# A transformer layer on eight cores: projection matmuls interleaved with attention at four per key block instead of two

## The reference

```python
x: (4, 4096, 1024) f32; 16 heads of 64; hidden 3072
Q, K, V = x Wq^T, x Wk^T, x Wv^T          # per head
S = Q K^T / 8, causal mask
O = softmax(S) V                          # blocked over keys, online in the reference
x = layernorm(x + O Wo^T)
h = silu(x Wg^T / 127) * (x Wu^T / 127)   # int weights
x = layernorm(x + h Wd^T / 127)
```

## Time and profile before

| | us |
|---|---|
| median of 3 runs | 2137.75 |
| lowest and highest | 2129.0, 2195.58 |
| the profiled execution | 2132.75 |
| its span, slowest core (core 5) | 2131.7 |
| spans of the other cores | 2101.8 to 2123.6 |
| granted TensorE clock, mean by core | 0.861 to 0.870 |

### The profile page before, as it was taken

One profiled execution on the slowest core, in us unless ns is written; L12 is line 12 of the kernel. 1 busy time (PEld: TensorE's weight loads), 2 busy tenths in 40 slices (PEclk: granted clock), 3 DMA queues, 4 the chain that ended last, 5 costly groups with the idle time before them and its releaser, 6 DMA issues. The chain is left out here.

```text
span 2131.7 us, 22780 instructions; the slowest of 8 cores (2101.8 to 2131.7 us)
## 1 busy us (share of the span) xinstructions
PE 1649.6 (77%) x7240; PEld 603.1 (28%) x7240; DVE 613.1 (29%) x1436; ACT 825.4 (39%) x999; POOL 183.9 (9%) x221
## 2 busy tenths in 40 slices
PE   3857989678888678888667775677899889998872
PEld 1512222212223222223111111222344334443320
DVE  1333132252332252322431222264311112111224
ACT  0025768156775067773237664133111011112012
POOL 1010000100000200000000000001122011221000
PEclk9967999869999679999558787787999999999985
DMA  7691122642123702215100000424679666777622
GB/s 101 108 128 21 21 41 39 93 59 40 21 41 55 102 14 41 40 21 81 21 1 1 1 1 2 121 72 45 60 70 86 58 65 58 72 72 68 93 55 79
DMA packets 224112, 115.31 MB, mean 54 GB/s; under 512 B 152030, under 2 KB 215520, under 8 KB 224000
## 3 DMA queue, kind: packets, MB, share of 16 engines
q0 software_dynamic: 215104, 96.94, 37.4%
q1 hardware_dynamic: 8896, 16.91, 2.3%
HBM read 201.66 MB, written 8.65 MB: 99 GB/s over the span
## 5 line engine op out<-in xcount | busy, mean ns | idle before, releaser
L415 ACT ACTIVATE pt<-sp,cbias 128x1024 bf16<-128x1024 f32 (+3 forms) x640 | 620.4, 986 | 271.3 <-PE sp L403 257.9
L443 PE MATMUL op<-pt,vbuf 128*65 128x512 bf16 (+3 forms) x1280 | 375.0, 377 | 136.6 <-DVE pt L424 60.8
L398 PE MATMUL sp<-qbuf,kbuf 64*128 64x512 bf16 (+3 forms) x640 | 239.9, 384 | 2.1 <-DVE cbias L324 2.1
L403 PE MATMUL sp<-qbuf,kbuf 64*128 64x512 bf16 (+3 forms) x640 | 240.1, 384 | 0.0
L899 PE MATMUL dps<-hbuf,wdd 128*128 128x512 bf16 x768 | 178.8, 391 | 35.6 <-DVE y L910 34.4
L841 PE MATMUL gps<-x1b,wgb 128*128 128x512 bf16 x768 | 185.0, 384 | 22.5 <-DVE x1b L809 13.0
L443 PEld LDWEIGHTS op<-pt,vbuf 128*65 128x65 bf16 x1280 | 109.4, 116 | 298.6 <-issue 269.4
L850 PE MATMUL ups<-x1b,wub 128*128 128x512 bf16 x768 | 183.8, 383 | 6.8 <-DVE hbuf L862 6.8
L226 PE MATMUL pp<-xstg,wkb 128*128 128x512 bf16 x512 | 153.4, 410 | 45.3 <-DMA xstg<-xfm 39.8
L240 PE MATMUL pp<-wvb,xstg 128*128 128x256 bf16 x1024 | 174.1, 281 | 0.8
L858 ACT ACTIVATE sgb<-gps 128x512 bf16<-128x512 f32 x96 | 57.3, 597 | 300.6 <-PE gps L841 291.2
(11 more groups left out here) (83 smaller groups left out, 1219.7 us busy)
## 6 DMA issues: line engine op xcount, KB each, us to landing
xstg<-xfm POOLq DMA_DIRECT2D x32, 1024.0 KB, 9.2
xstg<-xq POOLq DMA_DIRECT2D x16, 1024.0 KB, 9.5
wgb<-wgT POOLq DMA_DIRECT2D x48, 256.0 KB, 4.7
wub<-wuT POOLq DMA_DIRECT2D x48, 256.0 KB, 5.5
wdd<-wdT POOLq DMA_DIRECT2D x16, 768.0 KB, 10.1
xres<-xq SPq DMA_DIRECT2D x32, 256.0 KB, 3.1
yout<-y SPq DMA_DIRECT2D x4, 2048.0 KB, 6.9
wqb<-wqT POOLq DMA_DIRECT2D x4, 512.0 KB, 10.6
```

The source lines that it names most:

```text
L398: nc.tensor.matmul(sp[buf][:, js * 128: 512], kbuf[pb][0:64, hp * T + kb * 128: hp * T + kb * 128 + 128], qbuf[pb][0:64, hp * TOWN + qbase ...
L403: s_s.inc(nc.tensor.matmul(sp[buf][:, 512 + js * 128: 1024], kbuf[pb][64:128, hp * T + kb * 128: hp * T + kb * 128 + 128], qbuf[pb][64:128 ...
L415: s_exp.inc(nc.scalar.activation(pview, sview, AF.Exp, bias=cbias[pb][:, 0:1]))
L443: lastpv = nc.tensor.matmul(ops[hl][:, js * 128: 512], vbuf[pb][:, kb * VGW + (2 * hp + hl) * 65: kb * VGW + (2 * hp + hl) * 65 + 65], pt[ ...
```

## The change

The number of generator steps taken in each slot goes from 2 to 4. Nothing else differs; every instruction is still there, in another order.

```diff
@@ -499,7 +499,7 @@
             if p >= 1:
                 parts.append(norm_gen(p - 1))
             filler = chaing(*parts) if parts else None
-            filler = attention_pass(p, filler, rate=2)
+            filler = attention_pass(p, filler, rate=4)
             if filler is not None:
                 for _ in filler:
                     pass
```

## The result

The changed kernel takes 2079.62 us (median of 10), the kernel before 2140.79 (median of 10); the ratio is 0.9743, with a 95% interval of 0.9715 to 0.9771, so it is 2.6% faster. The profiled execution of the changed kernel took 2079.08 us. Where a sentence on core 5 compares both kernels, its spans are 2076.3 after and 2131.7 before. Some executions of an eight-core program are a few per cent longer whatever the kernel; ratios leave them out, and where a time is called "about", a median holds such executions, and the ratio times 2139, the middle of the medians of the kernel before in the experiments (2138.0 to 2140.6), stands in its place.

The account below looks back on a forecast made before the run. Slots with K or Q fillers were taken as bound by PE, the others by ACT. Passes 0 to 2 with their tails gain 11.3, 7.3 and 6.7 us, pass 3 loses 1.5: -24, 2110 us said, range 2076 to 2144.

Parts of the forecast that it names:

- rival of a larger gain: Fillers in PE's idle time keep the clock full, diagonal V slots stay 1.05, no x waits: -60, 2073 us; chance 0.24.
- The tail: Between passes: 2.9 us of DVE copies, 25.1 of the bound c, up to 1 waiting for late loads; together 29.
- Pass 3: Last attention pass, only the normalisation as filler: two more yields in its first slot put PV behind the wait, +1.5 us.
- The normalisation: Slots 112 to 114 of passes 1 and 2: 7.3 us wait, 23.3 in all against 22.9 in the tail; no gain.
- Bank starts: Each bank's first slot, where PE waits 3.1 us for DVE's copies: two more fillers are hidden there at present price.
- Full V slots: Non-diagonal slots with V fillers at rate 4: 1.335 us each, now bound by PE; 34 a pass counted.
- Diagonal slots: Last 8 slots of each bank at rate 4: K or Q 1.47 us, V 1.18 with 0.1 added for mask waits.
- Loss at the half clock: Passes take 13 us more than their count, mostly stretches at 1.2 GHz after idle bank starts; left as it is.
- x tiles: Key tile loads hidden; the first Q tile's load makes PE wait about 3 us a pass, between 0 and 14.
- theory A: Gain beyond the forecast is half-clock time PE no longer loses, since fillers fill the idle time at bank starts.
- rival of displaced work: The 128 yields cost 23 us in either place; diagonal V slots cost 1.35: 2127 to 2145 us; chance 0.21.
- The slower one: Granted clock in the dense 112 slots falls to a mean near 0.80: +48 us, 2181; chance 0.08.

Follow-up runs that it names:

- e11: e7 with three x buffers in place of two, and the normalisation issued early in parts, its write and reloads by SP; 1935 us, ratio 0.9046.
- e4: Kernel before (2 fillers a slot), but 8 fillers in each bank's first slot; 2081 us, ratio 0.9748 to the kernel before.
- e2: Changed kernel with 6 fillers a slot in place of 4; about 2135 us, ratio 0.998 to the kernel before.
- e7: Changed kernel with fillers given out by PE time per slot (full 0.32 us, diagonal 0.46, bank's first 2.2) instead of by number; 2005 us, ratio 0.9379.
- e9: e5 with the normalisation's write and reloads issued by SP instead of POOL; about 2060 us, ratio 0.9635 to the kernel before.
- e5: Changed kernel with the normalisation taken apart: transfers in the second key tile, broadcasts singly, one every 8 steps; 2086 us, ratio 0.9766 to the kernel before.
- e8: e7 with the normalisation taken apart, still on POOL, broadcasts one every 16 steps, allowances 2.4 and 0.52; 2011 us, ratio 0.9419.

## Why the forecast was right or wrong, step by step

The direction was right and the time, 2079.6, is within the stated range, near its low end. The likeliest case, -24 us and 2092 to 2125, did not come, and the forecast had put 0.66 on a change within 2% and only 0.26 on a faster kernel. The measured -55 is close to the rival of a larger gain (-60), so the range holds the result by that rival's share in it, not by the sum. By its steps, on core 5:

- *The tail*, 28 to 29 us: right, 27.8 to 28.1. The 1 us wait for late loads did not come.
- *Pass 3*, +1.5: right, +1.1.
- *The normalisation*: right. PE waits 6.73 us where 7.3 was said, and bank 2 with it takes 59.1 us in pass 1 against 35.6 in pass 0, 23.5 where 23.3 was said. Moved as a block it gains nothing; e11 shows that it gains when taken apart.
- *Bank starts*: right. From the end of one bank's last product to the next bank's first are 3.1 us as before (238.74 to 241.83), with four fillers hidden in them.
- *Full K slots*: right, 1.72. *Full V slots*: 1.30 instead of 1.335, which is 34 x 0.04 = 1.4 us a pass.
- *Diagonal slots*: the term that was mis-sized. Bank 2 of the first pair takes 35.0 us at clock 1.00; without 7 x 1.72 + 1.29 + 8 x 1.30 + 2.9 = 26.6 there are 8.4 for 8 V slots, 1.05 each, what a slot costs at rate 2, not 1.18. Bank 3 gives in the same way 9.7 for 4 K and 4 V slots, so a K slot is 1.38, not 1.47. Together 27 x 0.13 + 19 x 0.09 = 5.2 a pass. 1.05 is also the forecast's own PE work of such a slot, 0.60 and the 0.45 measured for four V fillers, so no wait for the mask was left on top; the 0.1 put on top had no row behind it.
- *Loss at the half clock*, left at 13 us a pass: wrong in place, and too high. With the terms above the count of a pass is 233.6 - 1.4 - 5.2 = 227.0; pass 0 took 239.5, so 12.5 are left, 3.5 of them waits for x. So 9 us against the 13 kept. This 9 is a remainder, not a measured time. The stretches at the half clock add up to about as much as before, 29.4 us of pass 0 against 30.5 (granted mean 0.93 in both); what changed is where they stand. Banks 2 and 3 of the first pair have none now. Bank 3 of the second pair, without fillers, has 10 us of them and takes 40.2 us, where the count of its bare slots is 24 x 1.16 + 8 x 1.05 + 2.9 = 39.1: in slots bound by ACT they cost 1 us. The largest piece of the 9 is in the bank where the Q tiles begin, 31.9 - 24.2 - 2.86 = 4.8 us. The forecast also priced the loss of the kernel before twice, at 13 us in its sum and at 7 to 8 in the rival of a larger gain; e4 puts it near 10.
- *x tiles*, 3 us: 2.86 + 0.65 = 3.5 measured in pass 0. As a wait right. The bank takes 31.9 us where the count with the new terms gives 24.2; the rest is the half clock that the point above has, of which 3.4 us follow the wait and 6.8 the bank's start.

Pass 0 by terms: 6.6 less from the slots, 3.9 less from the clock, 0.5 more for x, 10.0 in all. The three passes were 10.0, 10.6 and 8.6 us shorter than said (249.5, 273.0, 270.8), and each tail 1 us: 32 us on these stages of core 5, against the 30 between 2109 and 2079. So theory A alone, which put all of it on the clock, was too strong for the changed kernel: more than half (6.6 of the 10.0 in pass 0) is diagonal slots and V fillers, as far as the two banks read stand for all. The clock is decisive for the kernel before, where e4 wins it back.

The rival of displaced work failed at its first step, diagonal V slots of 1.35. The slower one needed a mean clock near 0.80 in the dense stretch; it was 1.00 in two of its banks and 0.84 in the worst. Of the larger gain's three items, diagonal V slots at 1.05 came (3.5 us a pass), the clock came in part (3.9 of 5 to 6), and the waits for x, which it had at nothing, stayed. That its total was nearly met is in part luck: K slots in the diagonal and the V fillers made up for the x tiles.

The forecast set a third level of the clock aside by the earlier trace rows. The profiled execution of the changed kernel agrees with it; that of e2 does not, as the last section shows.

## What to carry to other kernels

Filler work should be given out by the time that each slot has to spare, not by number: here 0.3 us in a slot bound by ACT, more in a diagonal one, over 2 us at a bank's start, and with that a pass that holds its whole projection took less time than one that held five sevenths of it. Before a change of rate is costed, read from one bank at full clock what its slots take, and price time at the half clock apart, with the place that causes it. No run gave a fixed number to the slots and more to the bank starts at a rate that leaves no tail, so how much of e7's gain is the filling of bank starts and how much the pacing inside them is not shown. A small chain of transfers moved earlier belongs on a queue where no large load stands behind it.

## What the runs showed of the hardware

- In twelve of the thirteen profiled executions TensorE's granted clock took only its two levels, 1.2 and 2.4 GHz, with all eight cores in dense matmuls: banks at 1.00 for 35.0 and 46.7 us, PE busy 95 and 96%. The thirteenth, that of e2, has a third level. Windows of e2: core 0, then the same stretch on core 5.
```profile
170.00:290.00 120.00, 117.08 (x607) 53.98 (x607) 36.62 (x96) 60.75 (x61) 6.99 (x8) 0.81 0.40 63
...
170.00:290.00 120.00, 111.17 (x663) 53.81 (x662) 40.72 (x108) 65.52 (x66) 7.86 (x9) 0.98 0.47 73
```
  There cores 0 and 1 were granted 0.81 in this stretch, cores 2 and 3 in a later one (from 1850 to 1970 us), cores 4 to 7 never. Eight matmuls of 512 columns took 2.10 us on core 3 at 0.81 and 1.73 on core 4 at 1.00. The Trainium skill (TensorE: Matmul & The Clock Gate, Part 1) expects this level, 13/16, for a die of which three cores or more run dense matmuls. The trace of e2 agrees with the level; the other twelve, with the same load, do not show it, so the load alone does not bring it here.
- At the bank starts of passes 0 to 2 on core 5, idle time of 2.0 to 2.8 us was followed by half clock at 18 of 21 in the kernel before and at 10 of 15 in the changed one; with 0.7 to 1.6 us idle it was at none of 23 (6 in the changed kernel, 17 in e4). The same page (Why this matters for your kernels) names idle of PE between bursts of matmuls as what brings the lower level back; at these starts the trace agrees in kind, though not every time. The stretch of e9 in the next point it does not explain: in the 20 us before it PE was idle for 0.89 us at most.
- The f32 broadcasts, which use 2 of 128 rows, ran at half clock for 13.99 us back to back. In e9 core 5 stayed at 0.50 for 27.3 us in which PE was busy for 26.15, eight such matmuls among them, while core 7 kept 1.00 over most of the same instructions. So here a busy PE did not bring the full level back. How densely the broadcasts stand may matter: in e5 and e9, with one every 8 steps, between 1 and 8 of a pass's 16 such matmuls ran at half clock on every core; in e8 and e11, with one every 16 steps, none of 512 did. But e8 and e11 are also paced, and the spacing was not tried alone, so whether these matmuls are the cause is not shown.
- V matmuls of 256 columns stand 0.11 us apart inside a slot (0.45 for four) and 0.12 in a long run of their own.
